# Two-layer graph network with residuals and layer norms: the counting sort's 1000-wide picks written one step of four columns ahead, in eight buffers in place of four

## The reference, cut to what matters

```python
edge_index = jnp.stack([src, dst])
# layer 0: row, col = src, dst
msg = (x @ W_lin + b_lin)[col] + (edge_attr @ W_edge + b_edge)
x = _layernorm(x + relu(segment_sum(msg, row)))
# layer 1, three times: mean of u[src] over the edges of each (dst, type)
h = segment_sum(u[src], dst * 8 + etype) / max(count, 1)
u = einsum('nrf,rfo->no', h, W) + u @ root + bias      # relu between them
x = _layernorm(x + u)
```

## Time and profile before

| | us |
|---|---|
| median of 3 runs (lowest, highest) | 5284.67 (5283.87, 5290.28) |
| the profiled execution: its own time | 5296.44 |
| span of its core in the profile | 5294.7 |
| busy: TensorE, VectorE, GpSimd, ScalarE | 4173.4, 3672.2, 2660.8, 2158.7 |
| mean granted TensorE clock, share of full speed | 0.872 |

### The profile page before, as it was taken

How to read it: one execution, slowest core, us unless ns; L and a number is a source line. 1 busy time by engine, 2 the same in 40 slices (tenths; PEclk the granted TensorE clock), 3 DMA queues, 4 the chain that set the end, 5 groups by cost and what they waited for, 6 DMA issues and landing times.

```text
span 5294.7 us, 118295 instructions
## 1 busy us (share of the span) xinstructions
PE 4173.4 (79%) x30835; PEld 3240.1 (61%) x30836; DVE 3672.2 (69%) x8050; ACT 2158.7 (41%) x5004; POOL 2660.8 (50%) x2369
## 2 busy tenths in 40 slices
PE   3478888877888566666667888899988999988997
PEld 2445555555554455555454777776777777777776
DVE  8967777777777777777774566566566676566667
ACT  0014344444432111111113555576555576555575
POOL 3878788888700777777771000475000475000476
PEclk8557788888878778878886999999999999999999
DMA  1011111111100423223221455675455675455676
GB/s 40 28 44 37 40 40 40 40 41 39 32 0 0 104 74 77 74 73 77 74 74 10 145 171 170 180 208 162 135 171 172 184 208 168 131 172 172 183 208 182
DMA packets 672518, 553.38 MB, mean 105 GB/s; under 512 B 158723, under 2 KB 584885, under 8 KB 672462
## 3 DMA queue, kind: packets, MB, share of 16 engines
q0 software_dynamic: 111712, 277.47, 18.4%
q1 hardware_dynamic: 560750, 275.24, 17.9%
HBM read 307.55 MB, written 244.94 MB: 104 GB/s over the span
## 4 chain that ended last, share of the span: by engine, by line
PE 53%; issue 14%; POOL 14%; DVE 13%; DMA 4%; DVEq 1%; ACT 0%; POOLq 0%; SPq 0%; ACTq 0%
PE ps L799 24%; PE ps L796 23%; POOL y_sb L610 12%; DMA mid<-msgs,block_idx 4%; PE ps L1055 4%; DVE y_sb L1218 3%; DVE mid L1410 2%; DVE mid L1405 2%; POOL mid L622 2%; PE ps L894 1%; DVE mid L1379 1%; DVE mid L1371 1%; DVE y_sb L1245 0%; DVE mid L1583 0%; DMA y_sb<-in_x_dram,idx_st 0%
## 5 line engine op out<-in xcount | busy, mean ns | idle before, releaser
L796 PE MATMUL ps<-mid 128*128 128x128 f32 (+3 forms) x8452 | 1555.8, 320 | 333.0 <-DVE mid L1405 244.8
L634 ACT ACTIVATE mid<-ps 128x512 f32<-128x512 f16 (+4 forms) x2484 | 1084.8, 464 | 1400.2 <-PE ps L796 674.7
L622 POOL DMA_INDIRECT mid<-msgs,block_idx x750 | 715.4, 954 | 1748.7 <-DMA msgs<-mid 1501.3
L796 PEld LDWEIGHTS ps<-mid 128*128 128x128 f32 (+3 forms) x8452 | 919.8, 169 | 626.3 <-issue 298.7
L599 POOL DMA_INDIRECT slot_rows<-y_sb,row_st x784 | 1102.9, 1407 | 272.2 <-issue 230.2
L610 POOL DMA_INDIRECT y_sb<-in_x_dram,idx_st x808 | 824.9, 1021 | 528.2 <-ACT idx_st L634 279.3
L799 PE MATMUL ps<-y_sb,mid 128*128 x6552 | 945.8, 287 | 134.6 <-issue 132.7
L799 PEld LDWEIGHTS ps<-y_sb,mid 128*128 128x128 f32 x6552 | 793.9, 191 | 260.0 <-issue 213.7
L1583 DVE TENSOR_SCALAR mid<-iota,slot_lo,slot_w 128x128 f32<-128x128 f32 x2250 | 666.2, 379 | 311.8 <-PE ps L796 302.7
L799 PE MATMUL ps<-y_sb 128*128 128x193 f32 x1616 | 429.1, 421 | 280.3 <-DVE mid L1509 191.1
L634 ACT ACTIVATE y_sb<-ps 128x512 bf16<-128x512 f16 (+2 forms) x375 | 205.1, 554 | 1037.2 <-PE ps L976 888.2
(11 more groups left out here) (242 smaller groups left out, 3670.7 us busy)
## 6 DMA issues: line engine op xcount, KB each, us to landing
msgs<-mid SPq DMA_DIRECT2D x819, 256.0 KB, 2.3
y_sb<-slot_rows SPq DMA_DIRECT2D x101, 268.0 KB
y_sb<-in_edge_attr_dram SPq DMA_DIRECT2D x54, 256.0 KB
y_sb<-in_x_dram,idx_st POOLq DMA_INDIRECT x808
slot_rows<-y_sb,row_st POOLq DMA_INDIRECT x784
mid<-msgs,block_idx POOLq DMA_INDIRECT x750, 3.7
y_sb<-in_edge_attr_dram SPq DMA_DIRECT2D x44, 224.0 KB
mid<-in_L_gnn_W_dram SPq DMA_DIRECT2D x3, 512.0 KB
```

What stands on the lines that cost most here:

```text
L622: nc.gpsimd.indirect_dma_start(out=rows[:, s % RB, :], out_offset=None, in_=msg_blocks, in_offset=bass.IndirectOffsetOnAxis(ap=block_idx[: ...
L634: return nc.scalar.activation(o, i, func, **kw)
L796: return nc.tensor.matmul(o, a, b, start=False, stop=False, skip_group_check=True)
```

## The change

VectorE writes the picks of the *next* step of four columns at the very start of a step, ahead of taking what was looked up; those of step 0 of the next group are written at the start of step 3. Eight buffers take the place of four: four stay in `mid`, four (`more_hi`) lie in `y_sb` behind `bits_st`. The semaphore's start rises from 4 to 8 with them. The number of instructions of each kind, and their shapes, stay the same.

```diff
+        more_hi = [words(y_sb, at + b * HI // 2, HI // 2, BF16) for b in range(4)]
+        at += 2 * HI
...
-        pick_hi = take(4 * HI // 2, BF16).rearrange("p (b m) -> p b m", b=4)
+        pick_hi = [take(HI // 2, BF16) for _ in range(4)]
...
+        pick_hi += more_hi
...
-            pe.sem_inc(S["perm_used"], 4)
+            pe.sem_inc(S["perm_used"], 8)
...
-                            pick_hi[:, ci % 4, q * HI // 2:(q + 1) * HI // 2])
+                            pick_hi[ci % 8][:, q * HI // 2:(q + 1) * HI // 2])
...
+            def pick_place(g, par, b):
+
+                for i in range(4):
+                    ci = 4 * b + i
+                    c = GC * g + (ci - 2 * GC)
+                    dve.wait_ge(S["perm_used"], c + 1)
+                    v.tensor_scalar(pick_hi[ci % 8], iota_h[:, 0:HI], hi_f[:, par, ci:ci + 1],
+                                    mult[:, ds(c, 1)], ALU.is_equal, ALU.mult).then_inc(S["hi_picked"], 1)
+
             def sort_picks(g, par, pair, g0):
                 for b in range(GB):
+                    if b < GB - 1 and g0 >= 2:
+                        pick_place(g, par, b + 1)
+                    if b == GB - 1 and 1 <= g0 <= GROUPS:
+                        pick_place(g + 1, 1 - par, 0)
                     if g0 >= 1 and (b == 0) and g0 <= GROUPS:
                         take_looked(GB * g - 1, GB - 1, 1 - par)
                     if b and g0 < GROUPS:
                         take_looked(GB * g + (b - 1), b - 1, par)
                     if b == 0 and 1 <= g0 <= GROUPS:
                         place(g - 1, 1 - par)
-                    if g0 >= 2:
-                        for i in range(4):
-                            c = GC * g + (4 * b + i - 2 * GC)
-                            dve.wait_ge(S["perm_used"], c + 1)
-                            v.tensor_scalar(pick_hi[:, i, :], iota_h[:, 0:HI], hi_f[:, par, 4 * b + i:4 * b + i + 1],
-                                            mult[:, ds(c, 1)], ALU.is_equal, ALU.mult).then_inc(S["hi_picked"], 1)
                     if b == 1 and 1 <= g0 <= GROUPS:
                         dve.wait_ge(S["pos_step"], 7 * g)
-                        wait_used(dve, S["perm_used"], GC * g + (4 - 2 * GC) if g0 >= 2 else 0)
+                        wait_used(dve, S["perm_used"], GC * g + (8 - 2 * GC) if g0 >= 2 else 0)
...
-            dve.wait_ge(S["perm_used"], COLS + 4)
+            dve.wait_ge(S["perm_used"], COLS + 8)
```

## The result

| | before | changed | |
|---|---|---|---|
| median of 4 runs each, us | 5287.48 | 5163.85 | ratio 0.9761, 95% interval 0.9744 to 0.9778 |
| the profiled execution: its own time | 5296.44 | 5165.55 | |
| span of its core | 5294.7 | 5163.8 | -130.9 |
| last copy of the sort out of PSUM begins at | 1714.32 | 1583.66 | -130.7 |

A forecast was written before the change was run, and what follows sets the result against it. VectorE and TensorE waiting for each other bound the sort, 27.1 us a group; -21 up to turn 39 and -66 behind it give 5296.4 - 87 = 5209.4, the median 11.8 lower: 5197 us, 8-in-10 range 5152 to 5243.

The forecast's parts named there:

- The ping-pong and its end: In the sort, VectorE and TensorE wait for each other, 27.1 us a group; moving the picks removes both 2.3 us gaps.
- GpSimd takes over in the turns up to 39: In staging turns, ScalarE waits for landed scatters, so GpSimd's need of 26.9 us per 16 scatters sets the pace.
- Turn 39 starts at 1404.1, -21: In the sort, turn 39 waits for chunk 93's scatters and starts at 1404.1 in place of 1425.3 us: -21 us.
- the slower rival: In staging turns, scatters meet VectorE's blocks badly each time, 9.5 us of stretch: +23, 5308 us; chance 0.05.
- The free turns at 20.5, -66: From turn 39 to the sort's end nothing is staged; groups take 20.5 us, saving 66 us together.
- Nothing behind the sort moves: The stage after the sort starts that much earlier and is itself unchanged.
- The rule weighed: On scatters beside VectorE's work: tensor_tensor with both inputs in SBUF stretches them, picks (tensor_scalar) do not, nearly the skill's reverse.
- GpSimd not holding: In placing turns 2 to 38, scatters shrink to the group's 20.5 us, gaining 310 us: about 4975 us; chance 0.06.
- The slow tail: Behind turn 39, TensorE's clock keeps falling, about 24 us a group: -52, 5233 us; chance 0.13.
- Nothing moves: GpSimd already sets the sort's pace and ScalarE's table copies hold TensorE in the tail: 5280 us; chance 0.06.

The follow-up runs named there:

- step0_late: Changed kernel, but the picks of step 0 are written behind take_looked and place again, which moves those of step 1 behind place too: 5172.23 us, ratio 0.9775.
- tt_more: Changed kernel with four more tensor_tensor of 128 x 1000 per group on VectorE, into a buffer that nothing reads: 5290.25 us, ratio 1.0001.
- spread: Changed kernel with ScalarE's turns written out and its 80 chunks staged evenly over turns 0 to 47, not two in each of 0 to 39: 5065.8 us, ratio 0.9576.
- spread_lo_single: Changed kernel with staging spread over turns 0 to 47, and pick_dst and pick_lo each written as sixteen tensor_scalar per group: 4966.66 us, ratio 0.9382.

## Why the prediction was right, and where its sum was off

It said 5197 us, -87; measured are 5163.85, -124 (-131 between the two profiled executions). Step by step:

*The ping-pong and its end*: right. Both gaps are gone, no work was added, and the semaphore's new wait costs nothing that shows: in the free turns VectorE's picks wait 3.6 us in 152. `step0_late` puts a price on one of the gaps where nothing hides it, 4.3 us a group for a gap of 2.3; the rest is the clock at 0.50 behind it, as the rows had shown.

*GpSimd takes over in the turns up to 39, through ScalarE's `build_rows`*: right, and shown by four things: ScalarE's new wait of up to 5.8 us a turn; `step0_late`, where a gap costs nothing in these turns (though the stretch fell with it); `tt_more`, where they follow the stretch; and `spread`, which gains 98 us without touching VectorE or TensorE.

*Turn 39 starts at 1404.1, -21*: this is the step that came out wrong, as a size. Its waiting copies begin at 1369.68, -56. The term that was mis-sized is the stretch. My sum let the 76 chunks from 18 to 93 take 1030 us: 38 times 20.3 and 259 of stretch, which is 6.6 for each of the 39 groups that run beside them. They take 1368.4 - 371.4 = 997 us (from chunk 18's first scatter to chunk 93's last), so 226 of stretch, 5.8 a group: 33 us less. I had named the cause (each turn meets the scatters in a fixed place), and given it to the slower rival alone. It went the other way: the long scatters of over 5 us have gone. Both parts of the sum, this and the next, were too small, so the total is not right by two errors that cancel.

*The free turns at 20.5, -66*: right in kind, somewhat small. They take 19.6 us, VectorE's own work without any hand-over cost, and turn 48 takes 16.5. From the wait's end in turn 39 to the last copy are 214 us in place of 289, -75.

*Nothing behind the sort moves*: right, 3580.1 against 3580.4 us.

*The rule weighed*: on `tensor_tensor` the runs side with the rows. The Trainium skill ("SBUF — State Buffer", "Who interferes with whom") infers that a `tensor_tensor` does not hinder the writing of descriptors; here four of them put 1.8 us on 16 scatters, and with `pick_dst` taken away the stretch falls by 2.8. The same section of the Trainium skill also says, and the prediction left it out, that a VectorE instruction with two inputs in SBUF contends with a GpSimd instruction that reads SBUF; that would agree, but what a scatter reads there no run here shows. On `tensor_scalar` the prediction judged too early, from two scatters of 0.97 and 1.03 us. The same section of the Trainium skill says that `tensor_scalar` can run in a two-port mode, and that GpSimd is then blocked for the whole instruction if VectorE issues first; ten more of 128 x 1000 left the stretch of 16 scatters at 5.8 us, but beside four of them in a row 40 scatters of `spread_lo_single` took 0.8 to 1.0 us more, which goes the same way. A pick writes 1000 elements in 0.45 us and `pick_dst` 2048 in 2.2, so the picks run at 2.4 times its rate; which mode that is no run here shows.

*The rivals.* GpSimd not holding would have given 4975 us; it holds. The slow tail (24 us) did not come; VectorE is busy for 147 of 152 us there. The slower rival needed 29.2 us of GpSimd; `tt_more` shows what that looks like: at 28.1 us and 25.3 behind them the whole gain is gone (1.0001). "Nothing moves" falls with the result.

## What to carry to other kernels

When a wait is taken away in a loop, work out for every engine what a turn costs it alone, GpSimd's DMA issues included, and look for a buffer count that ties that engine to the loop: the gain ends at the next need, here 26.2 us and not 19.6. Then ask whether work that is staged for that engine can be spread over all turns; here this was worth another 98 us behind the change's 124, and 0.2% without the change. And an engine's need is not a constant: what another engine does beside it, and when, is part of its price.

## What the runs showed of the hardware that I had not expected

- VectorE's `tensor_tensor` with both inputs in SBUF stretches GpSimd's indirect DMA issue, by about 0.45 us for each 1.2 us instruction of `tt_more`. The price depends on where in a scatter it falls: with the same 9.6 us of it per group the stretch was 5.0 to 6.5 us in five orders of the same instructions.
- `tensor_scalar` of 128 x 1000 mostly costs a scatter little (1.03 us in place of 0.97 on average in the changed kernel), but not always: four in a row made 40 scatters of `spread_lo_single` take 1.75 to 1.96 us.
- Once the loop waits for GpSimd, it can lock to it: from `place` to `place` the turns 5 to 38 of the changed kernel take 26.2 or 26.3 us, all but two of 25.6, where before they ran from 24.8 to 30.0. It need not: `step0_late` waits for GpSimd too, and its turns run from 23.4 to 28.0.
- Sixteen `tensor_scalar` of 128 x 256 in f16 take 3.3 us, from start to next start, where two `tensor_tensor` of 128 x 2048 took 4.4, and they stretch the scatters less (3.0 in place of 5.8 per 16); at 128 x 128 that turns round (2.7 against 2.2).
